# Reordering the first third of a two-stage interaction kernel: load order, where the paired fields are spread, and x1 of chunk 5 ahead of A's first product

## The reference

```python
X0 = inputs.reshape(-1, 32, 64)            # inputs (512, 256) -> 64 samples, 32 fields, depth 64
Xi = X0
for W, b in ((W1, b1), (W2, b2), (W3, b3)):
    Wr = W.reshape(128, 32, m)             # m = 32, then 128, 128
    Xi = einsum('bhd,bmd,ohm->bod', X0, Xi, Wr) + b[None, :, None]
    pools.append(Xi.sum(axis=-1))
return concat(pools) @ fc_W.T + fc_b       # (64, 1)
```

## Time and profile before

| | |
|---|---|
| median of 3 runs | 81.9 us (81.87 to 82.09) |
| the profiled execution, its own time | 81.76 us |
| its span | 80.0 us, 1146 instructions |
| PE / PE weight load busy | 72.5 us (91%) / 51.6 us (65%) |
| DVE / ACT / POOL busy | 46.6 / 34.6 / 49.8 us (58% / 43% / 62%) |
| DMA | 12.01 MB, mean 150 GB/s |

### The profile page before, as it was taken

One profiled execution on the slowest core, in us unless ns is written; L12 is line 12 of the kernel. 1 busy time (PEld: TensorE's weight loads), 2 busy tenths in 40 slices (PEclk: granted clock), 3 DMA queues, 4 the chain that ended last, 5 costly groups with the idle time before them and its releaser, 6 DMA issues.

```text
span 80.0 us, 1146 instructions
## 1 busy us (share of the span) xinstructions
PE 72.5 (91%) x372; PEld 51.6 (65%) x372; DVE 46.6 (58%) x44; ACT 34.6 (43%) x51; POOL 49.8 (62%) x49
## 2 busy tenths in 40 slices
PE   4969499978999669999999999999999999999970
PEld 1315177843445356888888888888888888886840
DVE  1058699686859999289699819992003003213541
ACT  1833997279948956890864700552300300000000
POOL 4989846999994399738079989809955004162400
PEclk9999999999999999999999999999999999999999
DMA  1899999999995615439997000000000000000000
GB/s 22 250 362 266 368 370 351 381 386 390 372 330 163 189 37 135 117 69 381 394 335 307 12 4 0 4 0 0 0 0 0 0 0 0 0 8 0 0 0 0
DMA packets 7529, 12.01 MB, mean 150 GB/s; under 512 B 835, under 2 KB 3971, under 8 KB 7267
## 3 DMA queue, kind: packets, MB, share of 16 engines
q1 hardware_dynamic: 6915, 11.16, 40.8%
q10 hardware_dynamic: 608, 0.77, 3.1%
HBM read 10.88 MB, written 1.05 MB: 149 GB/s over the span
## 4 chain that ended last, share of the span: by engine, by line
PE 77%; DMA 7%; POOL 5%; ACT 3%; DVE 2%; issue 2%; SPq 1%; POOLq 0%; DVEq 0%
PE a_ps L581 28%; PE x_ps L581 25%; DMA w_sb<-w 7%; PE z_ps L575 6%; PE a_ps L674 5%; PE a_ps L636 2%; PE x_ps L609 2%; PE a_ps L635 2%; PE a_ps L647 2%; POOL w_sb L305 2%; POOL z_lo L309 2%; POOL xs L259 2%; DVE r_in L477 2%; PE a_ps L661 1%; PE x_ps L749 1%
## 5 line engine op out<-in xcount | busy, mean ns | idle before, releaser
L266 POOL TENSOR_TENSOR feat<-r_in,feat 128x1024 fp32r<-128x1024 f32 x8 | 19.2, 2403 | 4.6 <-ACT feat L360 4.1
L581 PE MATMUL x_ps<-feat,w_hi 128*128 128x512 f32 x64 | 19.0, 395 | 0.0
L581 PE MATMUL a_ps<-feat,a_hi 128*128 128x512 f32 x64 | 16.2, 395 | 0.0
L259 POOL TENSOR_TENSOR xs<-x_in,xs 32x512 fp32r<-32x512 f32 x7 | 10.8, 1548 | 7.6 <-ACT xs L360 7.3
L504 DVE SCALAR_TENSOR_TENSOR x<-a_ps,vec,x 128x512 f32<-128x512 f32 x7 | 5.2, 746 | 17.7 <-PE a_ps L636 17.7
L273 POOL TENSOR_TENSOR x<-x 128x512 f32<-128x512 f32 x6 | 7.8, 1292 | 10.7 <-DVE x L504 10.5
L581 PEld LDWEIGHTS x_ps<-feat,w_hi 128*128 128x128 f32 x64 | 11.9, 188 | 3.4 <-issue 0.8
L581 PEld LDWEIGHTS a_ps<-feat,a_hi 128*128 128x128 f32 x64 | 11.9, 188 | 2.7
L484 DVE TENSOR_TENSOR feat<-z_ps,feat 128x1024 fp32r<-128x1024 f32 x8 | 9.8, 1220 | 3.5 <-ACT feat L360 3.4
L360 ACT ACTIVATE feat<-z_ps 128x1024 fp32r<-128x1024 f32 x8 | 8.2, 1022 | 5.8 <-DVE z_ps L477 5.8
L581 PE MATMUL x_ps<-feat,w_lo 128*128 128x512 f32 x32 | 9.8, 391 | 0.0
(11 more groups left out here) (76 smaller groups left out, 74.7 us busy)
## 6 DMA issues: line engine op xcount, KB each, us to landing
w_sb<-w SPq DMA_DIRECT2D x9, 512.0 KB, 8.7
x_in<-xl SPq DMA_DIRECT2D x8, 256.0 KB, 7.3
r_in<-xr SPq DMA_DIRECT2D x2, 1024.0 KB, 6.0
a_by_fields<-at_sb SPq DMA_DIRECT2D x8, 96.0 KB, 2.1
x<-x ACTq DMA_DIRECT2D x1, 512.0 KB, 4.5
x<-x SPq DMA_DIRECT2D x1, 512.0 KB, 6.2
w_sb<-w SPq DMA_DIRECT2D x1, 256.0 KB, 11.6
a_by_fields<-at_sb SPq DMA_DIRECT2D x4, 64.0 KB, 2.1
```

Source lines behind the costliest of these rows:

```text
L259: nc.gpsimd.tensor_tensor(xs[rows, c, :], x_in[rows, c % X_BUFS, :], xs[rows, c, :].bitcast(f32), ALU.subtract).then_inc(xs_lo, 1)
L266: nc.gpsimd.tensor_tensor(feat[:, c, 1, of_half(1), :], z_of(c, 1), feat[:, c, 0, of_half(1), :].bitcast(f32), ALU.subtract).then_inc(lo_d ...
L581: nc.tensor.matmul(bank, weights[:, k, :], feat[:, c, part, k, :], start=(start and k == 0), stop=False)
```

## The change

- **Loads.** x16 moves from ACT's queue, where it was first, to SP's, as the seventh load. New SP order: x 0, W1, x 1, W3 0, x 2, W3 1, x16, x 3, W3 2, W3 3, W1's rest, W2 0, x 4, W2 1, W2 2, W2 3, x 5, x 6.
- **POOL.** The identity (memset and select) moves from before the spread weights to after split_x(1). W1's sum and split_x(1) stand ahead of the small copies from `vec`. lo(0) stands ahead of split_x(2). z16_lo moves behind lo(1). W1 rest's sum leaves POOL. b23 moves behind split_x(6).
- **DVE.** The pairs' product moves from ahead of mult(0,0) to behind chunk 1. W1 rest's sum comes in (`rest_sum`), between mult(3,0) and mult(3,1), with a semaphore of its own; lo(3) and rest_lo follow, then chunk 4 whole.
- **ACT.** z16_hi moves behind hi(1,1); hi(2,0), split_x(4), hi(2,1) stand ahead of v_st; save_zz(0) behind v_st; W1 rest's high part between hi(3,0) and hi(3,1); split_x(5) between save_a(0) and save_a(1); hi(4,0) ahead of save_a(2); save_zz(1) ahead of f2's DMAs.
- **PE.** spread16(0) moves from ahead of x1 of chunk 0 to between pick_right(3,0) and the last part of x1 of chunk 1, and waits for `v_saved` 3; v_part(0) no longer waits for `zz_saved`, a_round(0) does. keep_clock(6) becomes keep_clock(8). Both v_part(2) and (3) stand after pick_right(2,0); all of x1_hi(1) ahead of the transpose. x1_product(5) moves ahead of the q matmul and a_product(0) and (1), x1_product(6) ahead of a_product(2).

```diff
@@ SP
             load_w3(0)
+            load_x(2)
             load_w3(1)
-            load_x(2)
+            sp.dma_start(x16[:, :, :], bass.AP(x.tensor, 0, [[N, P], [HALF * COLS, 2], [1, N]])).then_inc(x16_in, 16)
+            load_x(3)
             load_w3(2)
             load_w3(3)
-            load_x(3)
+            sp.dma_start(w1_sb[:, :, EVEN:, :], w1[:, :, EVEN:, :]).then_inc(w1_rest_in, 16)
...
@@ POOL
-            nc.gpsimd.memset(ident[:, :], 0.0).then_inc(ident_done, 1)
...
+            pool.wait_ge(w1_in, 16)
+            nc.gpsimd.tensor_tensor(w1_sb[:, 0, 0:TILES, :], w1_sb[:, 0, 0:TILES, :], w1_sb[:, 1, 0:TILES, :],
+                                    ALU.add).then_inc(w_sum, 1)
+            pool.wait_ge(w_sum, 1)
+            pool.wait_ge(xs_lo, 1)
+            split_x(1)
...
+            nc.gpsimd.memset(ident[:, :], 0.0).then_inc(ident_done, 1)
...
+            lo(0)
+            pool.wait_ge(lo_done[1], 1)
             split_x(2)
             pool.wait_ge(xs_lo, 3)
-            lo(0)
-            pool.wait_ge(lo_done[1], 1)
             split_x(3)
             pool.wait_ge(xs_lo, 4)
             lo(1)
             pool.wait_ge(lo_done[1], 2)
+            pool.wait_ge(hi16_done, 1)
+            nc.gpsimd.tensor_tensor(z16_lo[:, :], x16[:, 0, :], z16_hi[:, :].bitcast(f32),
+                                    ALU.subtract).then_inc(lo16_done, 1)
...
@@ ACT
             hi(1, 1)
+            act.wait_ge(z16_done, 1)
+            copy(z16_hi[:, :], x16[:, 0, :]).then_inc(hi16_done, 1)
             act.wait_ge(vt_ready, 1)
             copy(vt_sb[:, :], vt_ps).then_inc(vt_saved, 1)
+            hi(2, 0)
+            split_x(4)
+            hi(2, 1)
             act.wait_ge(v_ready, 1)
...
-            hi(2, 0)
-            split_x(4)
-            hi(2, 1)
+            save_zz(0)
+            hi(3, 0)
+            act.wait_ge(w_rest_sum, 1)
+            copy(w1_hi[:, EVEN:, :], w1_sb[:, 0, EVEN:, :]).then_inc(w_hi_done, 1)
+            hi(3, 1)
             save_a(0)
+            split_x(5)
             save_a(1)
-            hi(3, 0)
+            hi(4, 0)
             save_a(2)
             save_a(3)
...
             save_x1(1)
+            save_zz(1)
             act.wait_ge(zeros_done, ZEROS)
             act.wait_ge(a_out, A_OUT)
...
@@ DVE
+            def rest_sum():
+                dve.wait_ge(w1_rest_in, 16)
+                nc.vector.tensor_tensor(w1_sb[:, 0, EVEN:, :], w1_sb[:, 0, EVEN:, :], w1_sb[:, 1, EVEN:, :],
+                                        ALU.add).then_inc(w_rest_sum, 1)
...
-            dve.wait_ge(x16_in, 16)
-            nc.vector.tensor_tensor(x16[:, 0, :], x16[:, 0, :], x16[:, 1, :], ALU.mult).then_inc(z16_done, 1)
             mult(0, 0)
             mult(0, 1)
             lo(0)
             dve.wait_ge(w_hi_done, 1)
             main_lo(w1_sb[:, 0, :, :], w1_hi, w1_lo, w_lo_done)
             chunk(1)
+            dve.wait_ge(x16_in, 16)
+            nc.vector.tensor_tensor(x16[:, 0, :], x16[:, 0, :], x16[:, 1, :], ALU.mult).then_inc(z16_done, 1)
             chunk(2)
-            chunk(3)
-            mult(4, 0)
-            mult(4, 1)
+            mult(3, 0)
+            rest_sum()
+            mult(3, 1)
+            lo(3)
...
@@ PE
-            keep_clock(6)
-            spread16(0)
+            keep_clock(8)
             x1_main(0, 0)
             pick_right(1, 0)
+            x1_main(0, 1)
             pick_right(1, 1)
-            x1_main(0, 1)
             x1_lo(0, 0)
+            v_part(0)
+            v_part(1)
             x1_low_weights(0, 0)
             x1_low_weights(0, 1)
-            v_part(0)
-            v_part(1)
+            x1_lo(0, 1)
+            pick_right(2, 0)
             v_part(2)
-            pick_right(2, 0)
+            v_part(3)
             pick_right(2, 1)
-            v_part(3)
+            x1_hi(1, 0)
+            x1_hi(1, 1)
             pe.wait_ge(ident_done, 2)
             pe.wait_ge(vt_saved, 1)
             nc.tensor.transpose(v_ps, vt_sb[:, :], ident[:, :]).then_inc(v_ready, 1)
-            x1_lo(0, 1)
+            x1_lo(1, 0)
             pick_right(3, 0)
+            spread16(0)
+            x1_lo(1, 1)
+            pick_right(3, 1)
             a_round(0)
             a_round(1)
-            x1_hi(1, 0)
-            pick_right(3, 1)
+            pick_right(4, 0)
+            pick_right(4, 1)
             a_round(2)
             a_round(3)
...
             x1_tail(0)
             x1_tail(1)
+            pick_right(5, 0)
+            spread16(1)
+            x1_hi(2, 0)
+            x1_lo(2, 0)
             pick_right(5, 1)
...
             x1_product(4)
+            x1_product(5)
             pe.wait_ge(v_saved, 4)
...
             a_product(0)
             a_product(1)
-            x1_product(5)
+            x1_product(6)
             a_product(2)
-            x1_product(6)
             a_product(3)
```

More of the change, by code:

```diff
@@ L131, in cin_kernel @@
         w_sum, w_hi_done, w_lo_done = sem("w_sum"), sem("w_hi_done"), sem("w_lo_done")
+        w_rest_sum = sem("w_rest_sum")
         f_sum, a_hi_done, a_lo_done = sem("f_sum"), sem("a_hi_done"), sem("a_lo_done")
@@ L286, in _ @@
             nc.gpsimd.memset(ones[:, :], 1.0).then_inc(ones_done, 1)
-            nc.gpsimd.memset(ident[:, :], 0.0).then_inc(ident_done, 1)
-            pool.wait_ge(ident_done, 1)
-            nc.gpsimd.affine_select(out=ident[:, :], in_=ident[:, :], compare_op=ALU.not_equal, fill=1.0,
-                                    base=0, pattern=[[-1, P]], channel_multiplier=1).then_inc(ident_done, 1)
             pool.wait_ge(spread_done, 1)
@@ L298, in _ @@
             nc.gpsimd.tensor_copy(spread[:, :, :].rearrange("p t c -> p (t c)"), r_in[:, 0, 0, :]).then_inc(spread_done, 1)
+            pool.wait_ge(w1_in, 16)
[4 more added lines that the diff above has]
+            split_x(1)
+            pool.wait_ge(xs_lo, 2)
             pool.wait_ge(vec_in, 16)
@@ L302, in _ @@
             nc.gpsimd.tensor_copy(v_st[:, FC2_COL:FC2_COL + 1], vec[:, 4:5]).then_inc(fc2_done, 1)
[L303 to L314, removed]
+            nc.gpsimd.memset(ident[:, :], 0.0).then_inc(ident_done, 1)
+            pool.wait_ge(ident_done, 1)
+            nc.gpsimd.affine_select(out=ident[:, :], in_=ident[:, :], compare_op=ALU.not_equal, fill=1.0,
+                                    base=0, pattern=[[-1, P]], channel_multiplier=1).then_inc(ident_done, 1)
+            lo(0)
+            pool.wait_ge(lo_done[1], 1)
             split_x(2)
             pool.wait_ge(xs_lo, 3)
-            lo(0)
-            pool.wait_ge(lo_done[1], 1)
             split_x(3)
@@ L325, in _ @@
             lo(2)
[L326 to L329, removed]
+            pool.wait_ge(lo_done[1], 3)
             split_x(5)
@@ L336, in _ @@
             split_x(6)
+            pool.wait_ge(xs_lo, 7)
+            nc.gpsimd.tensor_scalar(b23[:, :], vec[:, 1:3], float(D), 0.0, ALU.mult, ALU.add).then_inc(b23_done, 1)
             pool.wait_ge(xp_in, 16)
-            pool.wait_ge(xs_lo, 7)
             xp = x16[:, :, :].rearrange("p g (d b) -> p (g d) b", b=B)
@@ L390, in _ @@
             split_x(0)
-            act.wait_ge(z16_done, 1)
-            copy(z16_hi[:, :], x16[:, 0, :]).then_inc(hi16_done, 1)
             split_x(1)
@@ L397, in _ @@
             hi(0, 1)
-            save_zz(0)
             split_x(2)
@@ L433, in _ @@
                     scratch.tensor, (TILES * j + k) * M, [[(EXT + 1) * M, H], [1, (TILES - k) * M]])).then_inc(f_main_in, 16)
-            save_zz(1)
             hi(5, 0)
@@ L520, in _ @@
             chunk(1)
+            dve.wait_ge(x16_in, 16)
+            nc.vector.tensor_tensor(x16[:, 0, :], x16[:, 0, :], x16[:, 1, :], ALU.mult).then_inc(z16_done, 1)
             chunk(2)
-            chunk(3)
-            mult(4, 0)
-            mult(4, 1)
+            mult(3, 0)
+            rest_sum()
+            mult(3, 1)
+            lo(3)
             dve.wait_ge(w_hi_done, 2)
             rest_lo(w1_sb[:, 0, :, :], w1_hi, w_lo_done)
-            lo(4)
+            chunk(4)
             chunk(5)
@@ L642, in v_part @@
                     pe.wait_ge(window_done, 1)
-                    pe.wait_ge(zz_saved, 1)
                 pe.wait_ge(w3_in[n], 16)
@@ L656, in spread16 @@
                     pe.wait_ge(lo16_done, 1)
+                    pe.wait_ge(v_saved, 3)
                 else:
@@ L667, in a_round @@
                 if t == 0:
-                    pe.wait_ge(v_saved, 3)
+                    pe.wait_ge(zz_saved, 1)
                     pe.wait_ge(fc2_done, 1)
@@ L700, in _ @@
             nc.tensor.transpose(v_ps, vt_sb[:, :], ident[:, :]).then_inc(v_ready, 1)
-            x1_lo(0, 1)
+            x1_lo(1, 0)
             pick_right(3, 0)
+            spread16(0)
+            x1_lo(1, 1)
+            pick_right(3, 1)
             a_round(0)
             a_round(1)
-            x1_hi(1, 0)
-            pick_right(3, 1)
+            pick_right(4, 0)
+            pick_right(4, 1)
             a_round(2)
```

(10 more changed lines are left out.)

10 lines of the change are left out of this document (2 added, 8 removed).

## The result

Before: 81.88 us, the median of 14 runs (81.79 to 82.09). After: **83.56 us**, the median of 14 runs (82.21 to 83.97). The ratio is 1.0134 [1.0101, 1.0167]; it leaves out executions more than 1.5% above the kernel's own fastest, here nine of the fourteen, so the medians (83.56 / 81.88 = 1.0205) tell more. By either count the change makes the kernel slower, where I forecast 81.2.

The account below looks back on a forecast made before the run. PE was taken as the bound, full from about 28 us, with about 4.1 us of idleness before. Start 0.89 plus idleness 0.6, minus 0.15 and 0.6, gave 0.7 us earlier: 81.2 us, range 80.5 to 82.9.

Parts of the forecast that it names:

- the wait ahead of x1 of 4: Dense part: f2's loads on ACT delay hi(5,0) and save_x1(2), so chunk 4 starts at 36.5, 0.15 us lost.
- My 81.05: Forecast time of the profiled execution, 81.76 before, with the change 0.7 us faster; the median was put at 81.2.
- I take DVE first: Near 10 us: DVE's main_lo (9.89 to 10.57) runs before POOL's lo(0), ready at 9.93, which then ends at 12.95.
- x 1 at 6.4 us: Start: x 1 lands about 6.4, 1.2 behind W1 at 5.25, as x16 no longer shares the way.
- in time by 0.1: Start: ACT finishes split_x(1) and W1's high part at 7.5, before hi(0,0) is due at 7.63.
- x 4 at 18.3 us: Load of chunk 4 behind W3, taken as landing at 18.3; landing at 18.8 would cost up to 0.5 us.
- POOL wins at 9.9 us: Rival: POOL's lo(0) goes before main_lo, which ends at 12.9 instead of 10.57; 1.5 us slower, 82.7; chance 0.30.
- rest_sum, "hidden": DVE: rest_sum costs 0.4 and waits for POOL's split_x(4) to 21.35, covered since mult(3,1) cannot start before 22.2.
- A's round trip: A's stores and reloads: a_saved 4 at 28.3, first f1 load at 31.85, A's rest and a_lo about 41, before A(0) at 43.1.
- gap predicted 0.6: PE ahead of x1 of chunk 5: waits for save_x1(3), ending at 40.0 behind a_hi and f_sum; 0.6 us lost.

Follow-up runs that it names:

- a1_same: The changed kernel run again with nothing edited: median 83.33 us; its profiled execution took 83.60 us.
- a4: The changed kernel with POOL's lo(0) waiting for main_lo, and save_x1(3) ahead of the copy into a_hi on ACT: 82.12 us.
- b3: b2 with x1 of chunk 5 back behind A(1) and x1 of chunk 6 back behind A(2) on PE: 82.1 us.
- c1: b1 with save_x1(2) between hi(5,0) and hi(5,1) on ACT: 81.62 us.
- a2: The changed kernel with POOL's lo(0) waiting for main_lo, so DVE is always first there: 82.23 us.
- d2: The changed kernel with POOL's lo(0) back behind split_x(2), which waits for the long-done identity: 83.76 us.
- b2: The changed kernel with two POOL waits, lo(0) for main_lo and lo(2) for rest_sum; save_x1(3) not moved: 82.6 us.
- b1: b2 with save_x1(3) moved ahead of the copy into a_hi on ACT: 81.83 us.
- a3: The changed kernel with DVE's main_lo waiting for POOL's lo(0), so POOL is always first there: 84.5 us.
- c3: c1 with v_st's copies ahead of split_x(4), z16_lo ahead of lo(1), and x1 of chunks 5 and 6 at their old places: 81.1 us.

## Why the prediction was wrong, step by step

**Where its sum stands.** Walked, x1 of chunk 5 ended at 43.07; in after at 44.21, 1.14 later. The parts by place: 0.76 at x1_hi(2,0) (30.71, not 29.95); the wait ahead of x1 of 4, 0.15; x1 of 5 from 3.6 behind that to 3.54, −0.06; x1 of 5 itself 3.26 from its start to its end by the chain, not 2.97: 0.29. My 81.05 and these 1.14 make 82.19; the profiled execution had 82.21. The 1.43 between the rows of after and a1_same come on top, and 83.62 is a1_same's 83.60 and the median's 83.56. So the usual execution stands 2.5 behind the walk (83.56 against 81.05), in two parts: the port, which costs 1.1 by the medians and up to 1.43 by the rows, and the 1.14 that even the best execution loses.

**The step that failed: "I take DVE first", on x 1 at 6.4 us, "in time by 0.1".** x 1 landed at 6.94 in after and at 6.69 to 7.62 in the eleven other profiles with this load order. ACT in after (start, duration), with the last row for x 4:

```profile
6.94 0.63 ACT L359 ACTIVATE xs<-x_in 128x512 fp32r<-128x512 f32 x1 [2.57 <-DMA x_in<-xl]
7.48 0.61 ACT L359 ACTIVATE w_hi<-w_sb 128x512 fp32r<-128x512 f32 x1
8.10 1.02 ACT L359 ACTIVATE feat<-z_ps 128x1024 fp32r<-128x1024 f32 x1
9.35 1.06 ACT L359 ACTIVATE feat<-r_in 128x1024 fp32r<-128x1024 f32 x1 [0.23 <-DVE r_in L475]
...
18.86 0.63 ACT L359 ACTIVATE xs<-x_in 128x512 fp32r<-128x512 f32 x1 [0.84 <-DMA x_in<-xl]
```

I scaled W1's landing to x16's 4.5 and kept the 1.2 of x 1 behind it. W1 came at 5.9 in after (its sum starts at 5.94), not 5.25. With x 1 late, ACT is the one that holds hi(0,0): then hi(0,1) follows at once, POOL's lo(0) can start 2.04 behind hi(0,0)'s start and DVE's main_lo 2.25 (a1_same: 8.52, 10.56, 10.77), so POOL wins by 0.21.

In after DVE won for a reason that I had not walked: mult(0,0) was late as well. PE and DVE there:

```profile
1.19 4.87 PE L570 MATMUL x_ps<-at_sb 128*128 128x512 bf16 x11 [1.19 <-DVE at_sb L511]
5.50 1.69 PE L580 MATMUL z_ps<-xs,pick 128*128 128x512 f32 x4
...
6.83 1.23 DVE L475 TENSOR_TENSOR z_ps<-x_in,z_ps 128x1024 f32<-128x1024 f32 x1 [1.53 <-PE z_ps L580]
```

and PE in a1_same:

```profile
1.19 3.98 PE L570 MATMUL x_ps<-at_sb 128*128 128x512 bf16 x11 [1.19 <-DVE at_sb L511]
5.45 1.17 PE L580 MATMUL z_ps<-xs,pick 128*128 128x512 f32 x4 [0.28 <-DVE xs L515]
```

The first four matmuls on real data took 1.69 instead of 1.17, behind eleven matmuls on zeros that ended at 6.06 instead of 5.17. hi(0,0) started 1.27 behind mult(0,0), as when DVE holds it; ACT had been free since 8.00 by the 1.06 that lie between split_x(1) and hi(0,0) in a1_same. mult(0,1) ended at 9.32, and hi(0,1) had to wait for it, the 0.23 in its row. Of the twelve profiles, hi(0,0) follows mult(0,0) by 1.26 to 1.27 in four (after, a4, b3, c1), the four in which the first four matmuls took 1.60 or more; by the rows DVE would lead in these alone. So after's best execution was won by a second delay, and that is luck. In such an order DVE leads by 0.12 (10.37 against 10.49); my walk had 0.04, since it put mult(0,1) 1.14 behind mult(0,0) where it is 1.27.

**The second step: x 4 at 18.3 us.** I gave it with its own bound ("18.8 costs up to 0.5"). It landed at 18.85. split_x(4), hi(2,1) and v_st follow, and spread16(0) starts at 20.80 instead of 20.2; at x1_hi(2,0) the lag is 0.76. The first x1 matmul was late too (9.27, not 8.75), but behind it PE waited 0.50 for v_st, so an earlier start alone would only have lengthened that wait.

**The choice between forecast and rival.** The rival "POOL wins at 9.9 us" named the place, the condition and the price (1.5; measured 1.1 by the medians, 1.43 between two profiles). I gave it 0.30. By my own walk the lead was 0.04 us, under an estimate of the landing whose bounds I had put 0.9 apart; a lead that small, lost with any delay of x 1, was no ground for calling the other case likelier. It had to be the forecast.

**rest_sum, "hidden".** The cover was right for the order I walked: in after rest_sum (21.55 to 21.97) ended 1.0 ahead of mult(3,1). But I looked only at split_x(4) on POOL. The next thing in POOL's queue is lo(2), starting 0.13 us behind rest_sum. If it is first, rest_sum is 2.3 to 2.6 long, and only that 1.0 covers it (the profiles of a2 and d2). It was a second rival that I did not list.

**A's round trip.** Walked about right in its pieces: twelve stores from 25.8 to 31.35, the loads at 32.7 instead of 31.85, of which 0.76 is the late start. SP's and ACT's load rows:

```profile
32.72 1.75 SPq L235 DMA_DIRECT2D f<-a_by_fields  x4
...
32.73 1.77 ACTq L431 DMA_DIRECT2D f<-a_by_fields  x4
```

hi(5,0) followed at 34.61, f_sum took 2.75 behind POOL's lo(5) as in the earlier trace rows, and A(0) never waited. **x1 of chunk 5**: gap predicted 0.6; in after the tail of x1 of 4 starts at 40.28, so x1 of 5 could at 40.51 and does at 40.95, 0.44 later, and with its restart 0.56; in the times 0.5 (b3 against b2) to 0.77 (b1 against b2).

**A term that I left out.** Every wait on PE costs its restart too. In dense flow two matmuls have their successor 0.46 behind them, behind a wait 0.58 (PE of after):

```profile
30.71 0.74 PE L586 MATMUL x_ps<-feat,w_hi 128*128 128x512 f32 x2 [0.35 <-ACT x L373]
31.29 0.62 PE L586 MATMUL x_ps<-feat,w_lo 128*128 128x512 f32 x2
31.75 0.62 PE L586 MATMUL x_ps<-feat,w_hi 128*128 128x512 f32 x2
```

0.12 us each, ahead of x1 of 2, of 4 and of 5. The last is in the 0.29 above. The other 0.16 of the 0.29 is a slip of mine in comparing: I set my walk, which goes by the starts of PE's rows, against 40.81 of the chain. PE's own row of before, the small matmul ahead of A(0), starts at 40.65 (in after at 44.05):

```profile
40.65 0.28 PE L724 MATMUL a_ps<-vec,v_rep 128*128 128x1 f32 x2
```

So before would have ended x1 of 5 at 43.62, not 43.78, and the walk promised 0.55 us, not 0.7. (The waits listed in it add up to 3.40, not 3.45.)

**The Trainium skill**, "SBUF — State Buffer", section "Who interferes with whom", held in every row of such a pair shown here: the instruction that starts second waits for the whole of the first, DVE behind POOL (2.73, 2.27, 2.62) and POOL behind DVE (lo(0) 2.82 in after). It was right to set it against this change; the fault was to let a lead of 0.04 us decide it.

**Still open**: why the landings scatter (x 1 by 0.9 us, x 4 by 0.6) and why PE is late with its first four matmuls in some executions (next section); neither was tried by itself. How many of after's thirteen usual executions lost which of the two places isn't known either; only a1_same's profile was seen.

## What to carry to other kernels

When a change makes two instructions on VectorE and GpSimd ready within a few tenths of a microsecond, and both use the shared port, the order is a part of the program: write it down with a semaphore, put the short one first, and check every such pair behind it, since moving one moves the next. In a walk through queues, a step with less slack than the uncertainty of a DMA's landing is not a step but a fork, and each branch has to be priced; here the late one was the usual one. A product moved ahead of another to hide its latency needs its own inputs in time: save_x1(3) was tied to the very data that the move was to wait for.

## What the runs showed of the hardware

- When a GpSimd and a VectorE instruction contend, the second ends its own length less 0.10 to 0.14 us behind the first's end (main_lo in a1_same: 0.55 behind, where it takes 0.68 alone). One that already waits is served next (a1_same: main_lo ahead of split_x(2)); one that a semaphore frees at the first's end can lose again to GpSimd's next instruction, by 0.03 us (a3).
- x 1, the third load of one queue, landed between 6.69 and 7.62 us in twelve profiles of near-identical programs. With 512 KB more on ACT's queue it landed at 8.14 (one profile), and the program's four times lay within 0.18 us.
- The first four matmuls on real data (pick_right of chunk 0) took 1.17 us in before, a1_same, a2, b1, b2 and c3, 1.69 in after and 2.02 in c1, with the granted clock shown as 1.00 in each. What differs is how long PE keeps the slower of two paces: the matmuls on zeros start 0.43 us apart at first, 512 columns at the lower of TensorE's two levels (1.2 and 2.4 GHz), and 0.22 apart later. In a1_same the last four (4.14, 4.35, 4.57, 4.79) have the faster pace; in after all eleven have the slower one, the last starts at 5.43, and the first real matmul stands behind it. In c1 the real ones have it too, up to 7.12. The granted clock as shown doesn't tell that; the distances of the starts do.
